# A transformer block on eight cores: layer norm steps spread over successive groups, and one matmul with ones per softmax total and per two query tiles

## The chip, the cores and the metric

One Trainium2 chip, eight cores. Each core takes one of the eight sequences (2048 tokens of width 2048) and all the weights, and runs the same program; no core waits for another. The metric is the time of one execution in microseconds, that of the slowest core. Lower is better.

## The reference

```python
xn = (x - mean) / sqrt(var + 1e-5)                 # x: (8, 2048, 2048)
Q = xn @ W_q; K = xn @ W_k; V = xn @ W_v           # 16 query heads, 4 key heads of 128
Qr, Kr = rope(Q), rope(K)
attn = softmax(Qr @ Kr.T / sqrt(128)) @ V; attn = attn @ W_o
gate = silu((xn @ w_gate) * s_gate)                # int8 weights, 2048 x 8192
up = (xn @ w_up) * s_up
ffn = ((gate * up) @ w_down) * s_down              # 8192 x 2048
out = x + attn + ffn
```

## The kernel before

The program is written out engine by engine. Each helper call appends an instruction, or a wait for a counter that another engine raises, to the list of one engine: "t" (TensorE, PE in the profile), "v" (VectorE, DVE), "s" (ScalarE, ACT), "g" (GpSimd, POOL, which also issues the casting weight loads) and "y" (SyncE, SP, which issues the other DMAs). Each engine takes its list strictly in order. Matmuls are recorded in two helper lines, L109 (inside a sum) and L113 (the last of a sum), so that a matmul is told by its tiles.

**Prologue.** The 2048 rows come in 16 tiles of 128 rows (`x_t`, four buffers). Of each, `ln_stats` (DVE, L368 and L371) takes mean and variance, `ln_scale` makes the factors (a square root on ACT at L377, a reciprocal and a product on DVE), `ln_apply` (ACT, L392) writes the normalised rows in bf16, and `ln_transpose` turns them into `xn`, features on partitions: 16 small matmuls against the identity into two PSUM banks `ps_t` (L405), which ACT (L413) or DVE (L411) copies out. `xn[t]` holds four such tiles, 512 tokens. `ln_stage(t, j)`, for j from 0 to 7, does this for the four tiles of one `xn[t]`: statistics in stages 0 to 3, factors for two tiles at a time, transposes in stages 4 to 7, each copied out by ACT alone.

Between the stages stand groups of 16 matmuls: `keys(t, g)` (one key head of 512 tokens, by `rotated`) and `v_rows(t, sub)` (128 tokens of V). `rotated` writes a bank; DVE multiplies it with the cosine and sine tables (L465 to L467), ACT squares it into `sqb` (L469), POOL adds the products into `kst` (L473), SP stores that. `norms` later issues one matmul of `sqb` with a matrix of ones into `ps_m` (the squared length of each token's vector, on all partitions) and a DVE maximum over it (L446): an upper bound for the softmax exponent. `v_rows` writes a half of `ps_s`, ACT copies it to one of two `vst` buffers (L489), SP stores it. After the first four key groups come 28 groups with the stages of tiles 8 to 15 between the first 16; then 64 query groups (16 heads of four 512-token tiles) with the same `rotated`.

**Main part.** Two passes over 1024 tokens each. In a pass the feed-forward network, in products of eight matmuls (`ps_f`, seven products for each 2x2 block product), is the outer loop. DVE and ACT combine and evacuate the products, POOL and DVE make the weight operands; `add_operands` (POOL, L299) is a load that adds to what is there, and waits for the load before it. Between the matmuls `attention` takes steps, STEPS of them over each pass, evenly by the count of matmuls. A softmax tile has eight steps: two score matmuls (`ps_s`), one exponential of 128x1024 on ACT (L990), two matmuls with V. The exponentials are summed in `acc`, by DVE in steps 1 and 2 and by POOL in steps 3 to 7 (L1007). At step 7 `split` (POOL) adds the halves of `acc` (L951), casts the result to bf16 (`hi`, L953) and takes the remainder (`lo`, L955). During the next tile, at step 4, `total` sums over the partitions by two matmuls with ones (`hi`, then `lo`) into `ps_m`; DVE inverts at steps 4 and 5 and multiplies at step 6. The passes end with the output projection. In the trace the attention of the two passes begins at 457 and 1986 us, their output projections at 1769 and 3288 us.

## Time and profile before

| | |
|---|---|
| median of three runs | 3573.27 us (3490.6 to 3616.72) |
| the profiled execution, its own time | 3487.79 us |
| its span, slowest core | 3486.1 us (the eight cores: 3471.1 to 3486.1) |
| PE busy in the span | 98% |
| outside the span | 1.7 us |

The profile is that of the core whose span is longest. Sums below are made against the profiled execution.

### The profile page before, as it was taken

The page shows a single profiled execution, that of the slowest core. Times are in us where ns is not written, and L with a number is a line of the kernel's source. Part 1 is how long each engine was busy: PE and PEld are TensorE (multiplying, and loading weights), DVE is VectorE, ACT ScalarE, POOL GpSimd, SP SyncE. Part 2 cuts the span into 40 slices and gives each one's busy share as a digit, 9 for nine tenths or more (in the row PEclk, how much of TensorE's full clock was granted, in tenths as well). Part 3 has the DMA queues.
Part 4 walks back from the last instruction along what each step waited for, and adds up shares of the span by engine and source line. Part 5 has one row for each costly group of instructions (what it writes and reads, how often), then busy time and mean ns, then how long its engine had stood idle before and what let it go on. Part 6 is the DMA issues. An engine that isn't in the chain of part 4 may idle for free.

```text
span 3486.1 us, 49034 instructions; the slowest of 8 cores (3471.1 to 3486.1 us)
## 1 busy us (share of the span) xinstructions
PE 3399.9 (98%) x15824; PEld 1542.6 (44%) x15824; DVE 2391.4 (69%) x3226; ACT 1205.7 (35%) x1437; POOL 1624.7 (47%) x1521
## 2 busy tenths in 40 slices
PE   5899999999999999999999999999999999999999
PEld 2444444444444444444444444444444444444444
DVE  5468777767776777677743677677776777677633
ACT  4421133443334333443311133443344333433111
POOL 1134445555555555555511155555555555555311
PEclk9999999999999999999999999999999999999999
DMA  8555476698668776667697666676667666676864
GB/s 214 156 114 145 152 209 181 169 151 170 181 179 144 155 191 178 143 143 195 183 225 124 145 180 184 150 169 176 183 153 164 176 181 154 142 183 181 210 127 85
DMA packets 180568, 578.98 MB, mean 166 GB/s; under 512 B 28256, under 2 KB 54880, under 8 KB 176096
## 3 DMA queue, kind: packets, MB, share of 16 engines
q0 software_dynamic: 132768, 484.53, 60.2%
q1 hardware_dynamic: 47552, 91.32, 8.2%
q8 instruction: 134, 2.20, 0.3%
q14 instruction: 114, 0.93, 0.1%
HBM read 318.64 MB, written 109.05 MB: 123 GB/s over the span
## 4 chain that ended last, share of the span: by engine, by line
PE 89%; DMA 4%; DVE 3%; issue 2%; ACT 1%; POOL 1%; DVEq 0%; POOLq 0%; ACTq 0%; SPq 0%
PE ps_f L109 54%; PE ps_f L113 8%; PE ps_s L109 7%; PE ps_av L109 6%; PE ps_k L109 4%; PE ps_s L113 3%; PE ps_av L113 3%; PE ps_m L109 2%; DMA x_t<-x_nat 1%; DMA wab<-wd 1%; PE ps_m L113 1%; DMA outT<-ost 1%; DVE st L368 1%; POOL kst L473 0%; ACT expT L990 0%
## 5 line engine op out<-in xcount | busy, mean ns | idle before, releaser
L109 PE MATMUL ps_f<-xop,wab 128*128 128x512 bf16 x6272 | 1545.2, 379 | 15.4 <-DVE th L750 7.1
L990 ACT ACTIVATE expT<-ps_s,bias,isq_sb 128x1024 bf16<-128x1024 f32 x512 | 616.6, 1204 | 1092.9 <-PE ps_s L113 1043.3
L1007 POOL TENSOR_TENSOR acc<-acc,expT 128x1024 f32<-128x1024 f32 x320 | 688.5, 2152 | 634.9 <-ACT expT L990 581.4
L109 PEld LDWEIGHTS ps_f<-xop,wab 128*128 128x128 bf16 x6272 | 612.1, 98 | 761.2 <-issue 28.2
L109 PE MATMUL ps_f<-fop,wab 128*128 128x512 bf16 x3136 | 770.8, 380 | 12.9 <-DVE fop L766 4.5
L109 PEld LDWEIGHTS ps_f<-fop,wab 128*128 128x128 bf16 x3136 | 306.8, 98 | 386.4 <-issue 19.6
L113 PE MATMUL ps_f<-xop,wab 128*128 128x512 bf16 x896 | 339.6, 379 | 0.0
L814 DVE TENSOR_TENSOR ps_f<-ps_f,usum 128x512 f32<-128x512 f32 x384 | 264.8, 690 | 72.1 <-PE ps_f L113 64.9
L791 ACT ACTIVATE ost<-ps_f,sd_sb 128x512 f32<-128x512 f32 x256 | 174.5, 686 | 306.6 <-DVE ps_f L814 195.4
L822 DVE TENSOR_TENSOR usum<-usum,ps_f 128x512 f32<-128x512 f32 x384 | 260.0, 677 | 13.3 <-PE ps_f L113 13.1
L745 ACT ACTIVATE th<-ps_f,sgh 128x512 f32<-128x512 f32 x256 | 170.4, 686 | 229.5 <-DVE ps_f L814 194.9
L854 DVE TENSOR_TENSOR usum<-m2c,ps_f 128x512 f32<-128x512 f32 x192 | 131.0, 682 | 167.9 <-PE ps_f L113 145.8
L968 DVE RECIPROCAL ps_m<-ps_m 128x256 f32<-128x256 f32 x128 | 225.0, 1758 | 29.2 <-PE ps_m L113 28.7
L640 POOL DMA_DIRECT2D outT<-ost x127 | 112.0, 944 | 283.9 <-DVE ost L702 150.2
L750 DVE SCALAR_TENSOR_TENSOR th<-th,ps_f 128x512 f32<-128x512 f32 x256 | 170.2, 682 | 105.4 <-ACT th L745 103.2
L473 POOL TENSOR_TENSOR kst<-rpa,rpb 128x512 bf16<-128x512 f32 x80 | 111.3, 1395 | 281.3 <-DVE rpb L467 194.5
L850 ACT ACTIVATE m2c<-ps_f 128x512 f32<-128x512 f32 x192 | 114.4, 596 | 320.8 <-PE ps_f L113 262.3
L862 DVE TENSOR_TENSOR usum<-usum,ps_f 128x512 f32<-128x512 f32 x192 | 131.5, 685 | 135.1 <-PE ps_f L113 132.2
L311 DVE TENSOR_TENSOR wab<-wab 128x1024 bf16<-128x1024 bf16 x192 | 192.5, 1003 | 40.1 <-DMA wab<-wd 25.9
L766 DVE SCALAR_TENSOR_TENSOR fop<-ps_f,sgu,th 128x512 bf16<-128x512 f32 x256 | 188.9, 744 | 25.9 <-PE ps_f L113 9.7
L113 PE MATMUL ps_av<-expT,vt 128*128 128x512 bf16 x512 | 194.3, 379 | 0.0
L109 PE MATMUL ps_av<-expT,vt 128*128 128x512 bf16 x512 | 194.3, 379 | 0.0
(116 smaller groups left out, 3782.9 us busy)
## 6 DMA issues: line engine op xcount, KB each, us to landing
wab<-wg POOLq DMA_DIRECT2D x299, 512.0 KB, 4.9
wab<-wu POOLq DMA_DIRECT2D x296, 512.0 KB, 4.9
wab<-wd POOLq DMA_DIRECT2D x146, 512.0 KB, 4.8
outT<-ost POOLq DMA_DIRECT2D x127, 512.0 KB, 7.7
x_t<-x_nat SPq DMA_DIRECT2D x16, 1024.0 KB, 9.2
wo_sb<-wo POOLq DMA_DIRECT2D x32, 512.0 KB, 9.4
ring<-wq POOLq DMA_DIRECT2D x16, 512.0 KB, 7.8
q_scr<-kst SPq DMA_DIRECT2D x64, 128.0 KB, 2.8
```

What stands on the lines that cost most here:

```text
L109: streams["t"].append(lambda t, o=out, l=lhsT, r=rhs, a=start, z=stop: t.matmul(o, l, r, start=a, stop=z, skip_group_check=True))
L113: return op("t", lambda t, o=out, l=lhsT, r=rhs, a=start, z=stop: t.matmul(o, l, r, start=a, stop=z, skip_group_check=True))
L311: build = lambda v: v.tensor_sub(w[:, WS1], w[:, W11], w[:, W22])
L745: tanh = op("s", lambda s: s.activation(th[k][:], src[:], AF.Tanh, scale=sgh[:, ic:ic + 1]))
L750: th_ready[k] = op("v", lambda v: v.scalar_tensor_tensor(th[k][:], th[k][:], 1.0, src[:], ALU.add, ALU.mult))
L766: th_free[k] = op("v", lambda v: v.scalar_tensor_tensor(fop[:, slot, i, :], src[:], sgu[:, ic:ic + 1], th[k][:], ALU.mult, ALU.mult))
L791: written = op("s", lambda s: s.activation(ost[b][:, tile, :], src[:], AF.Identity, scale=sd_sb[:, dc:dc + 1]))
L814: c = op("v", lambda v: v.tensor_tensor(ps_f[bank][:], ps_f[bank][:], U[:], sign))
L822: take = lambda v: v.tensor_sub(U[:], U[:], ps_f[bank][:])
L968: c["inverse"] = op("v", lambda v: v.reciprocal(ps_m[:, cols], ps_m[:, cols]))
L990: e = op("s", lambda s, kk=k, gg=g, rr=r, tt=t: s.activation(expT[:, kk, :], ps_s[:], AF.Exp, bias=bias[:, gg, rr, tt:tt + 1], scale=isq_s ...
L1007: summed = op(eng, lambda x, d=acc, o=one, kk=k: x.tensor_add(d[:], o, expT[:, kk, :]))
```

## The change

It has three parts.

**Layer norm and loads in the prologue.** `ln_stage` gives way to `look(i)` (statistics), `rows(i)` (factors and normalised rows) and `cols(i)` (transposes, copied out by ACT and DVE, a half each). They are placed one step per group in the order look, rows, cols of successive tiles. Factors are made for one tile at a time. The loads of tiles 8 to 11 are issued after the first two groups of the 28 instead of after each `ln_apply`, the load of V's weights waits for tile 5 instead of tile 7, and the tables for tokens 1024 and up are loaded later. `v_rows` has four `vst` buffers, and its copy and store stand ahead of the layer norm steps.

**Query norms.** For queries ACT squares the 128 rows of the bank in two halves of 64 rows, each into rows 0 to 63 or 64 to 127 of its own buffer by whether the tile is even or odd; POOL adds the two buffers once per two tiles; one matmul with `halves` (ones in the two diagonal 64x64 blocks) serves both. `finish_norms` puts the maxima back in place with four small DVE copies.

**Softmax totals.** At step 7 only the halves of `acc` are added (`fold`). In the next tile's step 1 ACT copies rows 64 to 127 of the sum beside rows 0 to 63 (`shift`), at step 2 POOL adds them and splits the 64 rows (`split`), at step 3 ACT copies `lo` into rows 64 to 127 of `hl` (`lower`), and at step 4 one matmul with ones takes both. STEPS is 263, for the three more steps at a pass's end.

```diff
-            def ln_stage(t, j):
...
-                if j >= 4:
-                    ln_transpose(i + j - 4, ("s", "s"))
...
+            def look(i):
+                def run():
+                    seen[i] = ln_stats(i)
+                return run
+            def rows(i):
+                def run():
+                    ln_apply(i, ln_scale(i // 2 % 2, i % 2, 1, seen[i]))
+                    if 8 <= i < 12:
+                        load_x(i + 4)
+                return run
+            def cols(i):
+                return lambda: ln_transpose(i, ("s", "v"))
...
-            ln_stage(1, 0)
-            ln_stage(1, 1)
-            keys(0, 0, [stage(1, 2), stage(1, 3)])
-            wait("g", x_loaded[7])
+            look(4)()
+            rows(4)()
+            keys(0, 0)
+            wait("g", x_loaded[5])
             wv_loaded = dma("g", l_wv, lambda g: g.dma_start(wv_sb[:], wvd))
-            keys(0, 1, [stage(1, 4)])
-            keys(0, 2, [stage(1, 5)])
-            ln_stage(1, 6)
-            keys(0, 3, [stage(1, 7)])
+            keys(0, 1, [cols(4), look(5)])
+            keys(0, 2, [rows(5), look(6)])
+            keys(0, 3, [cols(5), rows(6), look(7)])
+            rows(7)()
+            cols(6)()
+            cols(7)()
...
+            beside = {4: [look(8)], 5: [rows(8), look(9)], 6: [cols(8), rows(9), look(10)],
+                      7: [cols(9), rows(10), look(11)], 8: [cols(10), rows(11), look(12)],
+                      9: [cols(11), rows(12), look(13)], 10: [rows(13), look(14)], 11: [cols(12), rows(14), look(15)],
+                      12: [cols(13), rows(15)], 13: [cols(14)], 14: [cols(15)]}
             for n, (what, t, k) in enumerate(groups):
-                v_last = what(t, k, [stage(2 + n // 8, n % 8)] if n < 16 else ())
-                if n == 4:
-                    load_cs(2)
-                    load_cs(3)
-                if n == 11:
+                v_last = what(t, k, beside.get(n, ()))
+                if n < 2:
+                    load_x(2 * n + 8)
+                    load_x(2 * n + 9)
+                if n in (8, 13):
+                    load_cs(2 + n // 13)
+                if n == 13:
...
+                    k, at_ = (n * NT + t) // 2 % 2, t % 2 * 64
+                    wait("s", freed, sq_free[k])
+                    op("s", lambda s: s.activation(sqb[k][at_:at_ + 64, :], bank[0:64, :], AF.Square))
+                    squared = op("s", lambda s: s.activation(squ[k][at_:at_ + 64, :], bank[64:128, :], AF.Square))
...
+                if n >= G and t % 2:
+                    wait("g", squared)
+                    both = op("g", lambda g: g.tensor_add(sqb[k][:], sqb[k][:], squ[k][:]))
+                    behind.append((both, k, biggest, halves))
...
+            def fold(acc, summed):
                 wait("g", summed)
-                f = op("g", lambda g: g.tensor_add(acc[:, 0:TS], acc[:, 0:TS], acc[:, TS:]))
+                return op("g", lambda g: g.tensor_add(acc[:, 0:TS], acc[:, 0:TS], acc[:, TS:]))
+            def shift(c):
+                acc = c["acc"]
+                wait("s", c["sum"])
+                c["sum"] = op("s", lambda s: s.activation(acc[0:64, TS:], acc[64:128, 0:TS], AF.Copy))
+            def split(c):
+                acc = c["acc"]
+                wait("g", c["sum"])
+                f = op("g", lambda g: g.tensor_add(acc[0:64, 0:TS], acc[0:64, 0:TS], acc[0:64, TS:]))
...
+            def lower(c):
+                wait("s", c["low"], hl_free[0])
+                c["parts"] = op("s", lambda s: s.activation(hl[64:128, :], lo[0:64, :], AF.Copy))
...
-                mm(ps_m[:], ones[:], hi[:], True, False)
-                hl_free[0] = mm_last(ps_m[:], ones[:], lo[:], False, True)
+                hl_free[0] = mm_last(ps_m[:], ones[:], hl[:], True, True)
...
-            ending = {4: total, 5: lambda c: invert(c, 1), 6: normalise}
+            ending = {1: shift, 2: split, 3: lower, 4: total, 5: lambda c: invert(c, 1), 6: normalise}
```

How the instructions move, at three places. Numbers behind a name only tell buffers apart, and lines of the changed kernel lie higher (L405 becomes L411). First, PE in the first four key groups, before (`xn_tm0` is tile 4, `xn_tm1` tile 5):

```order
L109 MATMUL ps_k1<-xn0_70,ring2_54 128x512 x15
L113 MATMUL ps_k1<-xn0_70,ring2_54 128x512
L405 MATMUL ps_t0<-ident_sb_92,xn_tm0_65 128x128 x8
L405 MATMUL ps_t1<-ident_sb_92,xn_tm0_65 128x128 x8
L109 MATMUL ps_av<-xn0_70,ring3_55 128x512 x15
L113 MATMUL ps_av<-xn0_70,ring3_55 128x512
L113 MATMUL ps_m<-sqb0_86,ones_43 128x512
L405 MATMUL ps_t0<-ident_sb_92,xn_tm1_66 128x128 x8
L405 MATMUL ps_t1<-ident_sb_92,xn_tm1_66 128x128 x8
L405 MATMUL ps_t0<-ident_sb_92,xn_tm2_67 128x128 x8
L405 MATMUL ps_t1<-ident_sb_92,xn_tm2_67 128x128 x8
L109 MATMUL ps_k0<-xn0_70,ring4_56 128x512 x15
```

and in the changed kernel:

```order
L109 MATMUL ps_k1<-xn0_71,ring2_55 128x512 x15
L113 MATMUL ps_k1<-xn0_71,ring2_55 128x512
L411 MATMUL ps_t0<-ident_sb_97,xn_tm0_66 128x128 x8
L411 MATMUL ps_t1<-ident_sb_97,xn_tm0_66 128x128 x8
L109 MATMUL ps_av<-xn0_71,ring3_56 128x512 x15
L113 MATMUL ps_av<-xn0_71,ring3_56 128x512
L113 MATMUL ps_m<-sqb0_87,ones_43 128x512
L109 MATMUL ps_k0<-xn0_71,ring4_57 128x512 x15
L113 MATMUL ps_k0<-xn0_71,ring4_57 128x512
L113 MATMUL ps_m<-sqb1_88,ones_43 128x512
L411 MATMUL ps_t0<-ident_sb_97,xn_tm1_67 128x128 x8
L411 MATMUL ps_t1<-ident_sb_97,xn_tm1_67 128x128 x8
```

Tile 5's and tile 6's transposes stood ahead of the fourth key group (`ring4`); now they stand behind it. On SP over the same groups, before (`x_t0` to `x_t3` are tiles 8 to 11):

```order
L346 DMA sin_sb1_79<-sinT 128x512
L337 DMA x_t0_61<-x_nat 128x2048
L337 DMA x_t1_62<-x_nat 128x2048
L337 DMA x_t2_63<-x_nat 128x2048
L475 DMA k_scr<-kst0_88 128x512
L337 DMA x_t3_64<-x_nat 128x2048
L475 DMA k_scr<-kst1_89 128x512
L475 DMA k_scr<-kst0_88 128x512
L475 DMA k_scr<-kst1_89 128x512
```

and in the changed kernel:

```order
L352 DMA sin_sb1_80<-sinT 128x512
L492 DMA k_scr<-kst0_91 128x512
L492 DMA k_scr<-kst1_92 128x512
L492 DMA k_scr<-kst0_91 128x512
L492 DMA k_scr<-kst1_92 128x512
L563 DMA sg_sb_98<-sg 128x64
L563 DMA su_sb_99<-su 128x64
L563 DMA sd_sb_47<-sd 128x16
L492 DMA k_scr<-kst0_91 128x512
L343 DMA x_t0_62<-x_nat 128x2048
L343 DMA x_t1_63<-x_nat 128x2048
```

The loads of tiles 8 to 11 stood among the stores of the first key groups; now these stores and three small tables go first. Last, the end of a softmax tile. On POOL, before:

```order
L1007 TENSOR_TENSOR acc_0_125<-acc_0_125,expT_120 128x1024
L951 TENSOR_TENSOR acc_0_125<-acc_0_125 128x512
L953 CAST hi_127<-acc_0_125 128x512
L955 TENSOR_TENSOR lo_128<-acc_0_125,hi_127 128x512
L299 DMA wab0_59<-wg8 128x2048
L291 DMA wab1_60<-wu8 128x2048 x3
L299 DMA wab1_60<-wu8 128x2048 x2
L1007 TENSOR_TENSOR acc_1_126<-acc_1_126,expT_120 128x1024
```

and in the changed kernel:

```order
L1048 TENSOR_TENSOR acc_0_131<-acc_0_131,expT_126 128x1024
L977 TENSOR_TENSOR acc_0_131<-acc_0_131 128x512
L302 DMA wab1_61<-wu8 128x2048 x2
L294 DMA wab0_60<-wg8 128x2048 x3
L989 TENSOR_TENSOR acc_0_131<-acc_0_131 64x512
L991 CAST hl_133<-acc_0_131 64x512
L993 TENSOR_TENSOR lo_134<-acc_0_131,hl_133 64x512
L302 DMA wab0_60<-wg8 128x2048
L1048 TENSOR_TENSOR acc_1_132<-acc_1_132,expT_126 128x1024
```

The cast and the difference stood right behind the sum of the halves; now they stand five weight loads later, on 64 rows. On ACT over such a tile, before:

```order
L990 ACTIVATE expT_120<-ps_s,bias_50,isq_sb_47 128x1024
L945 ACTIVATE av_sb_129<-ps_av 128x512
L745 ACTIVATE th3_124<-ps_f3,sgh_44 128x512
L745 ACTIVATE th1_122<-ps_f0,sgh_44 128x512
L990 ACTIVATE expT_120<-ps_s,bias_50,isq_sb_47 128x1024
L745 ACTIVATE th2_123<-ps_f1,sgh_44 128x512
L990 ACTIVATE expT_120<-ps_s,bias_50,isq_sb_47 128x1024
L745 ACTIVATE th0_121<-ps_f2,sgh_44 128x512
L850 ACTIVATE m2c_109<-ps_f3 128x512
L990 ACTIVATE expT_120<-ps_s,bias_50,isq_sb_47 128x1024 x3
```

and in the changed kernel:

```order
L1031 ACTIVATE expT_126<-ps_s,bias_51,isq_sb_48 128x1024
L972 ACTIVATE av_sb_135<-ps_av 128x512
L1031 ACTIVATE expT_126<-ps_s,bias_51,isq_sb_48 128x1024
L984 ACTIVATE acc_0_131<-acc_0_131 64x512
L772 ACTIVATE th3_130<-ps_f3,sgh_45 128x512
L772 ACTIVATE th1_128<-ps_f0,sgh_45 128x512
L772 ACTIVATE th2_129<-ps_f1,sgh_45 128x512
L1031 ACTIVATE expT_126<-ps_s,bias_51,isq_sb_48 128x1024
L772 ACTIVATE th0_127<-ps_f2,sgh_45 128x512
L877 ACTIVATE m2c_115<-ps_f3 128x512
L1031 ACTIVATE expT_126<-ps_s,bias_51,isq_sb_48 128x1024
L998 ACTIVATE hl_133<-lo_134 64x512
L1031 ACTIVATE expT_126<-ps_s,bias_51,isq_sb_48 128x1024 x2
```

The copy of `acc` (L984, `shift`) now stands ahead of three tanh evacuations of the feed-forward network, and that of `lo` (L998, `lower`) behind another exponential.

## Rows read from the trace of the kernel before

**Rows 1.** The page, part 1: busy time of each engine, share, instructions

```profile
PE 3399.9 (98%) x15824; PEld 1542.6 (44%) x15824; DVE 2391.4 (69%) x3226; ACT 1205.7 (35%) x1437; POOL 1624.7 (47%) x1521
```

**Rows 2.** Windows: stretch; busy of PE, PEld, DVE, ACT, POOL; clock; DMA share, GB/s

```profile
31.12:71.69 40.57, 26.06 (x131) 12.96 (x131) 20.70 (x40) 17.63 (x17) 3.05 (x3) 0.79 0.88 228
71.69:196.81 125.12, 111.25 (x589) 53.29 (x590) 57.96 (x104) 48.38 (x56) 21.41 (x21) 0.96 0.57 148
196.81:436.37 239.56, 236.88 (x1097) 107.10 (x1096) 189.22 (x262) 47.34 (x70) 99.62 (x80) 1.00 0.51 137
436.37:1770.00 1333.63, 1316.37 (x6071) 593.61 (x6072) 975.48 (x1287) 511.40 (x601) 723.09 (x665) 1.00 0.73 175
1970.00:3290.00 1320.00, 1308.95 (x6057) 591.44 (x6056) 976.02 (x1287) 514.17 (x603) 722.34 (x664) 1.00 0.68 174
```

**Rows 3.** Timeline of PE, 49 to 140 us: start, duration, line, tiles, [idle before]

```profile
49.57 1.86 PE L405 MATMUL ps_t<-ident_sb,xn_tm 128*128 128x128 bf16 x16 [8.86 <-ACT xn_tm L392]
...
71.69 3.40 PE L109 MATMUL ps_k<-xn,ring 128*128 128x512 bf16 x15 [1.73 <-ACT xn L413]
...
104.04 0.61 PE L405 MATMUL ps_t<-ident_sb,xn_tm 128*128 128x128 bf16 x8 [4.79 <-ACT xn L413]
...
126.98 5.77 PE L109 MATMUL ps_s<-wv_sb,xn 128*128 128x512 bf16 x15 [4.38 <-ACT vst L489]
...
139.71 1.06 PE L405 MATMUL ps_t<-ident_sb,xn_tm 128*128 128x128 bf16 x16
```

**Rows 4.** Timeline of DVE and ACT, 43 to 60 us

```profile
43.24 2.47 DVE L368 BATCH_NORM_STATS2 st<-x_t 128x6 f32<-128x512 f32 x4 [9.52 <-DMA x_t<-x_nat]
...
46.17 0.30 ACT L377 ACTIVATE std<-mv,eps_sb 128x2 f32<-128x2 f32 x1 [15.73 <-DVE mv L371]
...
49.84 2.41 DVE L368 BATCH_NORM_STATS2 st<-x_t 128x6 f32<-128x512 f32 x4
...
53.63 0.68 DVE L465 TENSOR_TENSOR rpa<-ps_k,cos_sb 128x512 f32<-128x512 f32 x1
...
53.86 2.09 ACT L392 ACTIVATE xn_tm<-x_t,nmr,rstd 128x2048 bf16<-128x2048 f32 x1 [0.86 <-DVE nmr L383]
...
57.95 0.69 DVE L446 TENSOR_REDUCE kmaxs<-ps_m 128x1 f32<-128x512 f32 x1
...
58.33 1.93 ACT L413 ACTIVATE xn<-ps_t 128x1024 bf16<-128x1024 bf16 x2
```

**Rows 5.** Timeline of ACT, around 126 us

```profile
126.24 0.60 ACT L489 ACTIVATE vst<-ps_s 128x512 bf16<-128x512 f32 x1 [8.47 <-DMA v_scr<-vst]
```

**Rows 6.** Timeline of PE, 428 to 437 us: end of the query projections

```profile
428.58 3.40 PE L109 MATMUL ps_k<-xn,ring 128*128 128x512 bf16 x15
...
431.82 0.38 PE L113 MATMUL ps_k<-xn,ring 128*128 128x512 bf16 x1
...
436.37 0.38 PE L113 MATMUL ps_m<-sqb,ones 128*128 128x512 bf16 x1 [2.01 <-ACT sqb L469]
```

**Rows 7.** Groups by line and shape on POOL: busy, mean ns, idle before

```profile
L299 POOL DMA_DIRECT2D wab<-wu x112 | 98.2, 896 | 111.2 <-DMA wab<-wu 108.5 <-PE ps_f L113 2.7
...
L951 POOL TENSOR_TENSOR acc<-acc 128x512 f32<-128x512 f32 x64 | 87.8, 1372 | 9.2
...
L955 POOL TENSOR_TENSOR lo<-acc,hi 128x512 bf16<-128x512 f32 x64 | 76.7, 1199 | 9.3
```

**Rows 8.** Timeline of POOL and ACT, 926 to 944 us: end of a softmax tile

```profile
926.91 1.27 POOL L951 TENSOR_TENSOR acc<-acc 128x512 f32<-128x512 f32 x1
...
932.63 1.20 ACT L990 ACTIVATE expT<-ps_s,bias,isq_sb 128x1024 bf16<-128x1024 f32 x1 [2.78 <-PE ps_s L113]
...
942.35 1.21 ACT L990 ACTIVATE expT<-ps_s,bias,isq_sb 128x1024 bf16<-128x1024 f32 x1
```

**Rows 9.** Waits of PE, 197 us to the end: total, times, longest

```profile
PE ps_f L109 <- DVE th L750: 10.3, 11, 1.6
...
PE ps_m L113 <- ACT sqb L469: 2.7, 2, 2.0
```

More of the change, by code:

```diff
@@ L225, in build_program @@
         l_kst = lanes("kst", 2)
-        l_vst = lanes("vst", 2)
+        l_vst = lanes("vst", 4)
         l_spill = lanes("spill", 2)
@@ L614, in finish_norms @@
                 wait("v", m_free[0])
+                for t in range(2):
+                    for k in (0, 64):
+                        last = op("v", lambda v, a=64 * t, t=t, k=k: v.tensor_copy(
+                            qmaxs[k:k + 64, :, :, t::2], qmax2[a:a + 64]))
+                wait("v", last)
                 kmax_ready = op("v", lambda v: v.reduce_max(kmax[:], kmaxs[:], axis=AX.X))
```

70 lines of the change are left out of this document (30 added, 40 removed).

## The prediction

> **What bounds the kernel now.** I begin with the page's busy times: PE is busy for 3399.9 of 3486.1 us [rows 1], so two things only can shorten the run: fewer matmuls, and fewer of the 86 us in which PE stands still or runs at half its clock. The windows say where those are [rows 2]. From 31.12 to 71.69 us PE has work for 26.1 of 40.6 us, at a mean granted clock of 0.79. From 71.69 us, where the first key group of tokens 512 to 1023 starts, to 196.81 us, where the query projections start, it has 111.3 of 125.1 us at 0.96. In the query projections it is idle for 2.7 us of 239.6, in the two attention stretches for 17.3 and 11.1 us at full clock. So in everything behind 197 us PE is the bound and a matmul taken away is worth its own time; ahead of it, order is what matters. The timeline of PE names the waits of the prologue [rows 3]: 8.86 us ahead of tile 4's transposes, 4.79 us inside tile 9's, 4.38 us ahead of a V group that waits for `vst`.
>
> **A matmul's price.** Fifteen matmuls start at 428.58 and the closing one at 431.82 [rows 6]: 3.24 / 15 = 0.216 us from start to start. The 0.38 of a row is the modelled length, not the price. A group of 16 is 3.46 us.
>
> **Prologue to the start at 71.69.** Tile 4's transposes wait, before, for the factors of tiles 4 and 5 together, and tile 5 arrives at 43.24 [rows 4]. In the changed kernel tile 4 goes alone and that wait ends; but what is late next is tiles 5 to 7 themselves. The group that starts at 71.69 needs all four. From 43.24 the list of DVE holds up to tile 7's factors: three statistics (2.47 and an aggregate: 2.8 each, 8.4), three triples of rope products (0.68 x 3, 6.2), two maxima of 0.69 (1.4), one copy out of PSUM (0.7, taken like the maximum) and three sets of factors at 1.2 (0.30 for the root and 0.86 until the rows are written, 3.6) [rows 4]. Sum 20.3, so 63.5 us. Then ACT: tile 7's rows 2.09, the waiting half of tile 6's copy 0.97 (half of 1.93), tile 7's first transposes 0.5 and its copy 1.0: 68.1 us. Gain 3.6 us. Tiles 6 and 7 don't bind unless late: the statistics of tile 7 started at 49.84 with no idle ahead of it [rows 4], so it had landed, and DVE now asks for it at about 57.
>
> PE will have been nearly idle before 68.1, where it now comes from a busy stretch. The row nearest to this is the V group after 4.38 us of idle: its 15 matmuls took 5.77 against 3.40 us for 15 at full clock [rows 3, 6], so 2.4 us lost. I take 2.4 (between 0 and 3.4, the time at half clock of one more group). Net gain at the start 1.2.
>
> **71.69 to 196.81.** At full clock the work is 28 groups x 16 x 0.216 = 96.8, eight sets of transposes at 0.90 (the row has 1.06, less the 0.16 by which a modelled end passes the next start) = 7.2, and twelve norms of 0.216 = 2.6: 106.6 us of 125.1. The other 18.5 are waits (13.9 by the window) and half clock. What caused them: statistics ahead of the rope products of the same group, ACT doing both halves of a tile's copy, and `vst` blocked for 8.47 us behind the store queue [rows 5], where an x load stood before each store. All three go: four `vst` buffers, one DVE half, and in the V groups, which have no rope products, the statistics. What comes next is ACT: per group with transposes it now has the copy of V 0.60, a root 0.30, 0.86 until the factors are there, the rows 2.09 and half a tile 0.97, in all 4.82 us [rows 4, 5] against PE's 3.46 + 0.90 = 4.36. Eight such groups lose 0.46 each: 3.7 us. That gives 110.3, a gain of 14.8. Bounds: 18.5 if the buffers hide ACT, 7 if half of the old waits stay. The moved instructions cost SP little: the key stores now go ahead of tile 8's load, which is asked for at about 85 us and issued at about 76; a load of this size has all of DMA's share that V's weights left (V's weights start when tile 5 is there, not tile 7).
>
> **Query projections.** 32 norm matmuls fewer: 32 x 0.216 = 6.9 us. Added per query tile is one more ACT square (0.60, as for a copy of this width [rows 5]) and per two tiles one POOL add (1.37, the nearest row in rows 7, though that one is f32). ACT is busy for 47 and POOL for 100 of 240 us [rows 2], so with 38 and 44 more they fit. Two places lose: PE waits for `sqb` twice, 2.7 us in all [rows 9]. The last one, 2.01 us at the end of the projections [rows 6], now waits for a second square and the POOL add: 2.0 more. At the other, a bank is freed by the second square: 0.6 more. Sum: 6.9 - 2.6 = 4.3 (bounds 2 and 7).
>
> **Softmax totals.** 64 tiles x 0.216 = 13.8 us of PE. What is added is on ACT and POOL: per tile two ACT copies (0.6 each) and one POOL add (1.27 [rows 8]). ACT has 511 busy of 1334 us [rows 2] and 39 more, POOL 723 and 41 more. `shift` waits for the sum of the halves: this ends at 926.91 + 1.27 = 928.2, the exponential of step 1 at 933.8 [rows 8], 5.6 us later: never late. `lower` waits for `split`, which starts at about step 2's matmuls, 937, and takes 1.27 + 0.6 + 1.2 [rows 7, 8], to 940.1, against the end of step 3's exponential at 943.6: 3.4 us to spare. Behind these waits on ACT are the tanh evacuations, for which DVE and then PE wait. PE's own waits for that chain are 10.3 us in 11 places [rows 9]; a copy ahead of it lengthens it by 0.6, in a fraction of the tiles. I take 3 us (5 of 64 tiles lose 0.6; bounds -3, since the cast and difference no longer stand ahead of weight loads, and 19, half of the tiles). Net 10.8.
>
> **The sum.** 1.2 + 14.8 + 4.3 + 10.8 = 31.1 us off the profiled execution's 3487.8: **3457 us**, 0.9% less. I forecast for executions like the profiled one, which lies at the low end of the three runs shown (3490.6 to 3616.7); against their median of 3573 the same number would look like 3%, and that would be no effect of the change. The memsets of `halves` hide behind the first loads of x and `finish_norms`' four copies behind PE's first four banks; uncovered, the copies would cost less than four maxima, 4 x 0.69 = 2.8 us.
>
> **A rule beside the rows.** The sum of halves on POOL has a mean of 1.37 us over 64 [rows 7] and 1.27 us undisturbed [rows 8], so 0.10 us a piece goes to others, 6 us in all, in 28 us of PE's idle time. The Trainium skill, "SBUF — State Buffer", section "SBUF: two separate sides", has GpSimd and VectorE share a port pair by an exclusive lock: an instruction of VectorE with two SBUF inputs and one of GpSimd that reads SBUF don't overlap. By that rule alone every added POOL add could stop VectorE for its full length. The rows speak for a tenth of it. Were the whole length lost, 64 x 1.27 = 81 us would fall on DVE, which has 358 + 344 us free in the two stretches [rows 2]; if PE paid half, the time would be 3457 + 40 = 3497. I give this 2 in 100.
>
> **Rivals.** *The saved matmuls turn into waits.* ACT's copies stand ahead of the evacuations in half of the tiles and PE loses 0.6 in each: 19 us instead of 3, 3473. For it: PE already waits there in 11 places. Against: ACT is idle for 60% of these stretches. *The prologue gains less.* V's weights now load beside tiles 6 and 7, and DMA's share is already 0.88 there [rows 2]. If tile 7 comes at 69 us instead of by 49.8 (12 us after DVE asks for it), everything behind moves by 12: 3469. *More gain.* ACT's rhythm is hidden, the clock returns at once and POOL's relief takes waits away: 3.7 + 2.4 + 6 + 3 = 15 more, 3442. *Slower than before.* POOL takes its list in order, and L299's loads wait for the load before them, 108.5 us over 112 of them [rows 7], 1 us on average. Where `split` stands behind such a wait of more than the 3.4 us to spare, ACT stops in `lower`, and with it exponentials and tanh. It decides from 31 / 64 = 0.5 us per tile on; at 1 us per tile the time is 3457 + 64 = 3521. Against: it takes waits four times the mean in every tile.
>
> **How the numbers follow.** Forecast (3445 to 3466) 0.64, waits in the attention 0.14, less in the prologue 0.08, more gain 0.08, slower through POOL 0.04, the port 0.02. The range of 8 in 10 goes from 3438 (beyond the case of more gain) to 3479 (beyond the two that lose part). Two per cent, about what a measurement of this kernel can tell from no change, is 70 us: faster by that would need twice the forecast gain, 0.03; slower would need the stop in `lower` at 1.6 us or more per tile, 0.02; within it 0.95.
>
> **What the changed profile would show.** PE with 96 matmuls fewer and no wait ahead of tile 4's transposes; the group of tokens 512 on starting at about 68 us, its first matmuls at half clock; the query projections starting at about 180 us; one wait of about 4 us at their end; `ps_m<-hl` 64 times, no long wait of ACT for `lo`; PE idle in each attention stretch within a few us of 17 and 11. The prediction is wrong if the idle time of those stretches grows by more than 10 us each, or if the projections start after 187 us.

## The result, and the profile after

| | before | changed |
|---|---|---|
| executions, four each | 3487.89 to 3616.72 us | 3450.99 to 4023.58 us |
| median | 3531.93 us | 3645.41 us |
| ratio of comparable executions | | 0.9892, 95% interval 0.9863 to 0.9921 |
| the profiled execution | 3487.79 us | 3452.65 us |
| PE in its slowest core | 3399.9 of 3486.1 us | 3376.9 of 3451.1 us |

The change makes the kernel 1.1% faster, within the 2% that count as the same. In some executions of either kernel all cores of a die run at a lower granted clock (0.84 to 0.89 in the two of the changed one that took 3838 and 4024 us, by which alone the medians say the opposite), so the ratio leaves these executions out, "mean span" below takes only cores of a die whose clock was 0.994 or more, and "cores 4 to 7" below means these alone, because cores 0 to 3 of that chip had 0.986 to 0.995 with the kernel before as well. The changed kernel run again gave 3449.12 to 3450.84 us in four executions, ratio 0.989 (0.9875 to 0.9904).

The profile is that of core 1. First the page's busy times, as [rows 1]:

```profile
PE 3376.9 (98%) x15728; PEld 1531.9 (44%) x15728; DVE 2420.4 (70%) x3216; ACT 1317.8 (38%) x1623; POOL 1765.3 (51%) x1620
```

96 matmuls fewer, 23 us less of PE; ACT has 112 us more, POOL 141, DVE 29. The windows of the stages, columns as in [rows 2]:

```profile
31.31:68.36 37.05, 22.57 (x131) 11.92 (x132) 23.92 (x46) 15.47 (x16) 5.53 (x5) 0.79 0.81 176
68.36:180.20 111.84, 110.31 (x592) 52.81 (x593) 63.92 (x115) 41.49 (x52) 18.82 (x19) 0.98 0.79 187
180.20:416.00 235.80, 229.38 (x1058) 103.02 (x1057) 164.73 (x227) 83.28 (x131) 127.43 (x110) 1.00 0.55 138
416.00:1741.00 1325.00, 1311.37 (x6043) 591.32 (x6042) 1001.06 (x1295) 555.31 (x668) 779.98 (x698) 1.00 0.73 175
1941.00:3253.00 1312.00, 1300.89 (x6019) 587.59 (x6017) 994.29 (x1287) 554.95 (x666) 776.27 (x695) 1.00 0.70 175
```

PE's idle time is 14.5 us ahead of 68.36 (as before) and 1.5 us in the next stretch (before 13.9). The window of the query projections ends here at 416, ahead of their last norm at 420.62, while the one in [rows 2] ends with it. Cut as there, at 179.73, 420.62 and 1741, PE is idle for 9.6 us in the query projections (before 2.7) and for 10.4 in the first attention stretch (before 17.3); in the second it is 11.1 as before. The timeline of PE in the prologue, against [rows 3]:

```profile
40.54 1.06 PE L411 MATMUL ps_t<-ident_sb,xn_tm 128*128 128x128 bf16 x16
...
51.10 1.05 PE L411 MATMUL ps_t<-ident_sb,xn_tm 128*128 128x128 bf16 x16 [1.82 <-ACT xn_tm L398]
58.25 1.87 PE L411 MATMUL ps_t<-ident_sb,xn_tm 128*128 128x128 bf16 x16 [6.10 <-ACT xn_tm L398]
65.55 1.86 PE L411 MATMUL ps_t<-ident_sb,xn_tm 128*128 128x128 bf16 x16 [5.43 <-ACT xn L419]
68.36 5.97 PE L109 MATMUL ps_k<-xn,ring 128*128 128x512 bf16 x15 [0.94 <-DVE xn L417]
...
96.73 1.05 PE L411 MATMUL ps_t<-ident_sb,xn_tm 128*128 128x128 bf16 x16 [0.40 <-ACT xn_tm L398]
...
101.62 1.05 PE L411 MATMUL ps_t<-ident_sb,xn_tm 128*128 128x128 bf16 x16 [0.38 <-ACT xn_tm L398]
...
106.50 1.05 PE L411 MATMUL ps_t<-ident_sb,xn_tm 128*128 128x128 bf16 x16 [0.38 <-ACT xn_tm L398]
...
111.38 0.83 PE L411 MATMUL ps_t<-ident_sb,xn_tm 128*128 128x128 bf16 x12 [0.38 <-ACT xn_tm L398]
```

Tile 4's transposes at 40.54 wait for nothing. Those of tiles 5, 6 and 7 wait 1.82, 6.10 and 5.43 us: the wait has gone down the row of tiles. Tokens 512 to 1023 begin at 68.36 us, at half clock (granted 0.50 from 60 to 71.5 us, in the first eight of which PE was busy for 2.0; 15 matmuls in 5.97 us against 3.40). From 96.73 on, four transposes in a row wait 0.38 to 0.40 us each for the rows that ACT writes, 4.88 us apart; behind them PE waits for nothing until the query projections, whose first matmul is at 179.73. There (PE again, against [rows 6]):

```profile
206.06 3.40 PE L109 MATMUL ps_av<-xn,ring 128*128 128x512 bf16 x15 [1.34 <-ACT squ L483]
...
236.30 3.40 PE L109 MATMUL ps_k<-xn,ring 128*128 128x512 bf16 x15 [0.76 <-ACT squ L483]
...
420.62 0.38 PE L113 MATMUL ps_m<-sqb,halves 128*128 128x512 bf16 x1 [3.21 <-POOL sqb L489]
```

The first two are matmuls that wait for a bank which the second square (L483) frees; there are five of that kind, 4.4 us in all. The last is the closing norm behind POOL's sum, 3.21 us for 2.01 before. PE's waits and one of ACT's from 197 us on, as [rows 9]:

```profile
PE ps_f L109 <- DVE th L777: 11.9, 12, 1.8
...
PE ps_m L113 <- POOL sqb L489: 5.1, 4, 3.2
...
ACT hl L998 <- POOL lo L993: 3.9, 2, 2.0
```

**Stages, mean of eight cores.** The profiled execution of every run has a trace of each core. The stages below are read from PE's rows on all of them: the first matmul of the query projections; from it to their last norm matmul; from that to the first matmul of the second output projection. "Mean span" is over all executions of the run, with an uncertainty of 0.3 to 1.1 us, and is set against the same mean of the kernel before (3478.2 to 3480.3 us), for "changed" that of its one traced execution, for the others that of several on the same chip.

| kernel | query projections start | they last, to the last norm | attention, to the second output projection | mean span, difference |
|---|---|---|---|---|
| before | 194.0 | 239.6 | 2846.0 | |
| changed | 179.3 | 236.3 | 2829.4 | -35.4 |
| changed, again | 179.6 | 234.9 | 2829.1 | -37.5 |
| prologue alone | 179.8 | 239.9 | 2845.1 | -16.7 |
| query norms alone | 195.2 | 237.4 | 2846.6 | -3.1 |
| softmax totals alone | 194.3 | 239.6 | 2831.8 | -13.2 |

### The profile page after: what moved, and what is told of

Its sections match the earlier page's. It is cut to its first block, busy times and chain, and to the rows that moved or that the text cites. A ratio compares the mean times of both kernels' runs of the same rounds, so it can differ in the third digit from the quotient of the medians.

```text
span 3451.1 us, 49221 instructions; the slowest of 8 cores (3436.1 to 3451.1 us)
## 1 busy us (share of the span) xinstructions
PE 3376.9 (98%) x15728; PEld 1531.9 (44%) x15728; DVE 2420.4 (70%) x3216; ACT 1317.8 (38%) x1623; POOL 1765.3 (51%) x1620
## 4 chain that ended last, share of the span: by engine, by line
PE 93%; DVE 2%; DMA 2%; issue 2%; ACT 1%; POOL 1%; DVEq 0%; ACTq 0%; POOLq 0%; SPq 0%
PE ps_f L109 57%; PE ps_f L113 8%; PE ps_s L109 7%; PE ps_av L109 6%; PE ps_k L109 4%; PE ps_s L113 3%; PE ps_av L113 3%; PE ps_m L109 2%; DMA q_scr<-kst 1%; PE ps_m L113 1%; PE ps_t L411 0%; ACT xn_tm L398 0%; POOL kst L486 0%; DMA wab<-wd 0%; PE ps_k L113 0%
## 5 line engine op out<-in xcount | busy, mean ns | idle before, releaser
L1048 POOL TENSOR_TENSOR acc<-acc,expT 128x1024 f32<-128x1024 f32 x320 | 688.5, 2152 | 553.5 <-ACT expT L1031 512.6
L849 DVE TENSOR_TENSOR usum<-usum,ps_f 128x512 f32<-128x512 f32 x384 | 259.9, 677 | 11.0 <-PE ps_f L113 11.0
L800 DVE TENSOR_TENSOR fop<-fop 128x512 bf16<-128x512 bf16 x320 | 200.6, 659 | 6.7
L109 PE MATMUL ps_s<-qr,kr 128*128 128x512 bf16 x512 | 194.3, 379 | 0.8 <-ACT expT L1031 0.8
## 6 DMA issues: line engine op xcount, KB each, us to landing
x_t<-x_nat SPq DMA_DIRECT2D x16, 1024.0 KB, 10.8
```

The costliest lines, as they stand in the source:

```text
L109: streams["t"].append(lambda t, o=out, l=lhsT, r=rhs, a=start, z=stop: t.matmul(o, l, r, start=a, stop=z, skip_group_check=True))
L800: fop_ready[dst] = op("v", lambda v: v.tensor_tensor(fop[:, dst, i, :], fop[:, one, i, :], fop[:, two, i, :], how))
L849: take = lambda v: v.tensor_sub(U[:], U[:], ps_f[bank][:])
L1048: summed = op(eng, lambda x, d=acc, o=one, kk=k: x.tensor_add(d[:], o, expT[:, kk, :]))
```

## The experiments

### The three parts one by one

Each is the kernel before with one part of the diff and nothing else (STEPS 263 with the softmax part, 260 without).

> The prologue's part of the change alone (layer norm steps spread, loads in order of use, four vst buffers); query norms and softmax totals as before. If the parts add up, the query projections start 15 to 17 us earlier than before (medians over the cores) and nothing behind changes by more than 1 us: about 3472 us. Rival: part of the gain is given back later, because V's weights and the later x loads push the stores; then the projections start early and the end moves by less than 12 us.

Ratio 0.994 (0.992 to 0.9959), -16.7 us.

> The query norms' part alone. By the prediction 4.3 us less in the query projections (32 matmuls are 6.9 us, less 2.6 of longer waits): about 3484 us. By the profile of the changed kernel 2 to 3 us less, because PE waits for a bank until ACT's second square five times, where DVE adds the xn halves into xop, and for the last POOL add.

Ratio 0.9985 (0.9974 to 0.9997), -3.1 us.

> The softmax totals' part alone. By the prediction 10.8 us less (13.8 from 64 matmuls, less 3 for two more ACT copies per tile): about 3477 us. Rival: the copies cost nothing and POOL is relieved, since its cast and difference no longer stand ahead of the weight loads: 14 to 17 us less, about 3472 us.

Ratio 0.9954 (0.9938 to 0.997), -13.2 us.

The three add up to -33.0 us and the product of the ratios is 0.9879, against -35.4 and -37.5 us and 0.9892 for all together. By the ratios nothing is missing; by mean spans the sum is 2 to 4 us short, with an uncertainty of nearly 2. In the table each part moves its own column most, but the last two less than in the whole: the norms 2.2 us of 3.3 and 4.7, the totals 14.2 of 16.6 and 16.8. So no part costs another anything, and a small gain comes perhaps only in company; the waits in the attention, below, point that way. The prologue part is the largest, as forecast.

### Inside the prologue: buffers or order

The kernel before with four `vst` buffers and the copy of V ahead of the layer norm steps:

```diff
-        vst = [place("vst%d" % i, ...) for i in range(2)]
+        vst = [place("vst%d" % i, ...) for i in range(4)]
...
+                wait("s", done, vs_free[sub])
+                s_free[vb] = op("s", lambda s: s.activation(vst[sub][:], ps_s[:, vb, :], AF.Copy))
...
                 for f in between:
                     f()
-                wait("s", done, vs_free[vb])
-                s_free[vb] = op("s", lambda s: s.activation(vst[vb][:], ps_s[:, vb, :], AF.Copy))
```

> The kernel before with four vst buffers and the copy and store of V ahead of the layer norm steps, nothing else of the change. The wait of 4.4 us for vst goes, with it the half clock behind it (2.4 us): projections start 5 to 7 us earlier if that wait was last, less than 2 us if the layer norm of the next tiles holds PE instead.

Ratio 0.9977 (0.9964 to 0.999), -7.6 us; the projections start at 186.6 us, half of the part's gain. The other way round, the changed kernel with two buffers and the copy behind the steps:

> The changed kernel with two buffers for V rows instead of four, and with their copy and store again behind the layer norm steps: the order of layer norm steps and of loads alone. The buffers alone had moved the start of the query projections from about 196 to 187 us, the whole prologue part to 180. Theory (the two halves add): the projections start at about 188 us here, so 8 us of the 16 are lost and the ratio is 0.9892 + 0.0023 = 0.9915; PE waits again for vst. Rival 1 (with x loads out of the store queue the old buffers don't block any more): start near 181, ratio 0.9895. Rival 2 (both are needed, each wait takes the place of the other): start near 193, ratio 0.993.

Ratio 0.9929 (0.9913 to 0.9945). Of cores 4 to 7 the mean span is 35.2 us below before, and the projections start at 180.2 (the changed kernel's, on the same cores of its two traced executions, at 178.9 and 179.7). So rival 1 holds for the start, and the ratio's own size, nearer to rival 2, comes from cores 0 to 3: with the new order the buffers are worth 0 to 2 us. They are a second cure of the same wait: on the timeline of PE (core 5) one wait for `vst` of 0.86 us is left of [rows 3]'s 4.38.

```profile
106.17 1.05 PE L411 MATMUL ps_t<-ident_sb,xn_tm 128*128 128x128 bf16 x16 [0.38 <-ACT xn_tm L398]
...
111.05 1.05 PE L411 MATMUL ps_t<-ident_sb,xn_tm 128*128 128x128 bf16 x16 [0.38 <-ACT xn_tm L398]
...
116.42 3.40 PE L109 MATMUL ps_s<-wv_sb,xn 128*128 128x512 bf16 x15 [0.86 <-ACT vst L506]
```

Changed with the loads of tiles 8 to 11 issued after each tile's rows, as before:

```diff
-                    if 8 <= i < 12:
+                    if 4 <= i < 12:
                         load_x(i + 4)
...
-                if n < 2:
-                    load_x(2 * n + 8)
-                    load_x(2 * n + 9)
```

> The changed kernel with the x loads issued after each ln_apply again, as before, all else kept (steps, vst, V's weights). If the place of the loads matters by itself, the load of tile 8 and later stand ahead of V's weights and the key stores, kst is held and the projections start 3 us or more later than in the changed kernel (180 us). If the order of the steps and the vst buffers make the gain, the start of the projections stays within 1 us.

Ratio 0.9886 (0.9857 to 0.9914), mean span 3442.7 us, the changed kernel's 3442.5 to 3442.8. On cores 2 to 5 of its traced execution the projections start at 178.2 to 180.2 us, as the expectation without an effect has it (the other four cores can't be compared). The place of these loads is worth nothing; it was not combined with two buffers, so whether the loads would block those again stays open. What does bind is ACT. Both halves of a transposed tile copied by ACT, as before the change (`("s", "s")` in `cols`):

> The changed kernel with both halves of each transposed tile copied out by ACT, as before the change, where the change gives one half to DVE. My forecast had ACT as the next bound of the stretch (4.82 us per group against PE's 4.36). If that holds, 0.97 us more per group on ACT goes straight to PE in eight groups: 8 us later, query projections at about 188 us, ratio 0.9915. Rival: ACT is not the bound (PE waited for nothing between 112 us and the projections), four buffers give slack, and the cost is 0 to 2 us: ratio 0.989 to 0.9898.

Ratio 0.9916 (0.9897 to 0.9935); of cores 4 to 7 the mean span is 33.0 us below before, 2 to 4 us of the gain lost, and the projections start at 181.3. Between the two expectations, and the timeline of PE (core 5) shows why:

```profile
94.99 1.05 PE L411 MATMUL ps_t<-ident_sb,xn_tm 128*128 128x128 bf16 x16 [0.40 <-ACT xn_tm L398]
...
100.78 1.05 PE L411 MATMUL ps_t<-ident_sb,xn_tm 128*128 128x128 bf16 x16 [1.29 <-ACT xn_tm L398]
...
106.58 1.05 PE L411 MATMUL ps_t<-ident_sb,xn_tm 128*128 128x128 bf16 x16 [1.29 <-ACT xn_tm L398]
...
112.38 1.05 PE L411 MATMUL ps_t<-ident_sb,xn_tm 128*128 128x128 bf16 x16 [1.29 <-ACT xn_tm L398]
```

The groups are 5.80 us apart where they were 4.88: ACT's rhythm is the forecast's 4.82 plus the 0.97 of another half, so in these groups ACT does set the pace. But there are only four in a row with a wait, not eight, and 3 x 0.92 = 2.8 us is what is lost.

### Query norms: banks and the end

```diff
+                if n == G and t == 0:
+                    banks.extend([ps_s[:, 0, :], ps_s[:, 1, :]])
+                    bank_free.extend([(s_free[0],), (s_free[1],)])
```

> The changed kernel with five instead of three PSUM banks for the query groups (the two halves of ps_s, idle then, are added). If PE's waits for ACT's second square come from the banks, all of them go (4.4 us in five places in the changed kernel's trace) and the projections take 4 us less; waits for POOL's add stay. Rival: DVE's sums of xn are what is late, and the waits move to the norm matmuls: less than 2 us gained. About 3448 us or 3451.

Ratio 0.9884 (0.9855 to 0.9912), mean span 3440.2 us, 2.3 and 2.6 below the two runs of the changed kernel. The projections last 234.2 us, and no wait for `squ` is left on any core; in the changed kernel these waits are 2.4 us in the mean of eight cores, in its second run 1.5. So the gain is what these waits had cost, between the two expectations. Then also the last two tiles' norms one by one, with `ones`, as for keys:

> The changed kernel with five PSUM banks in turn in the query projections and with the norms of the last two query tiles taken alone, as for keys. Theory: what the query projections still lose is two things only, the bank that the second square frees late (2.3 us less with five banks) and the wait for the POOL add at their end (3.2 us where it was 2.0 before the change). Both gone, the projections last about 226.5 us against 230.1 and the ratio to the kernel before is 0.9883 (3447 us). Rival: the last wait is not the POOL add but whatever closes the projections (rope, store, maxima); then the wait of about 3.5 us stays and the ratio is that of five banks alone plus one matmul more, 0.9885 to 0.989.

Ratio 0.9907 (0.989 to 0.9925), -35.1 us by cores 4 to 7: no better than the changed kernel, and rather worse than five banks (-39.1). Neither expectation was right. The timelines of PE and DVE at the end (core 4):

```profile
412.63 0.38 PE L113 MATMUL ps_m<-sqb,ones 128*128 128x512 bf16 x1 [4.24 <-DVE qmaxs L452]
```

```profile
408.72 0.68 DVE L477 TENSOR_TENSOR rpb<-ps_s,sin_sb 64x512 f32<-64x512 f32 x1
409.44 2.32 DVE L653 COPY qmaxs<-qmax 64x16 f32<-64x16 f32 x12
411.79 0.69 DVE L452 TENSOR_REDUCE qmaxs<-ps_m 128x1 f32<-128x512 f32 x1
```

My edit put the twelve small copies of the maxima (L653, 2.32 us) between two maxima on DVE; there is one `ps_m`, and the last norm waits 4.24 us for it, on every core, for 3.21 in the changed kernel. The wait was replaced by one of my own making, so what the POOL sum costs at the end was not isolated.

### Softmax totals: the copies and the place

The copies on ACT twice each (128 instructions more, each waited for):

```diff
             def shift(c):
...
+                wait("s", op("s", lambda s: s.activation(acc[0:64, TS:], acc[64:128, 0:TS], AF.Copy)))
...
             def lower(c):
...
+                wait("s", op("s", lambda s: s.activation(hl[64:128, :], lo[0:64, :], AF.Copy)))
```

> The changed kernel with shift and lower each done twice on ACT (the second right behind the first, with a wait of ACT for itself), so 128 more ACT copies of 0.63 us and nothing else. If an ACT copy ahead of the tanh evacuations costs PE what the prediction took (3 us for 128), the attention takes 3 us more than in the changed kernel; if its cost was hidden in the 13.8 us of the saved matmuls and POOL's relief masked it, 6 to 8 us more: 3460 us; if ACT has room, the time is that of the changed kernel within 1 us.

Ratio 0.9895 (0.9872 to 0.9917), mean span 3444.1 +- 0.8, attention 2828.6 us for 2829.4 and 2829.1. By mean spans, 80 us more on ACT cost between nothing and 2.3 us (-35.2 us against the kernel before, for -35.4 and -37.5).

The kernel before with `split` at step 2 of the next tile and all else as it was (128 rows, two matmuls):

```diff
-            ending = {4: total, 5: lambda c: invert(c, 1), 6: normalise}
+            ending = {2: split, 4: total, 5: lambda c: invert(c, 1), 6: normalise}
```

> The kernel before, with only the place of the split changed: the halves are added at step 7, the cast to bf16 and the difference (128 rows, as before) come at step 2 of the next tile, no ACT copies, two matmuls with ones as before. If the relief of POOL is worth something by itself, PE's idle time in the attention falls and the time is 2 to 4 us less than before, and POOL waits less for the adding weight loads (190 us before). If only the matmuls count, the time is that of before within 1 us.

Ratio 0.9975 (0.9962 to 0.9988), -5.8 us without one matmul less. STEPS is 261 here for 260, which the diff does not show, so all steps of the attention lie a little differently between the matmuls. PE's waits between 440 and 3290 us, mean of eight cores, fall from 25.2 to 20.6 us. The adding loads (L299) can't be shown to be the reason: see the next run. It is the changed kernel with the split moved forward, from step 2 to step 0 of the next tile (and STEPS 261 for 263):

```diff
-            ending = {1: shift, 2: split, 3: lower, 4: total, 5: ..., 6: normalise}
+            def early(c):
+                shift(c)
+                split(c)
+            ending = {1: lower, 4: total, 5: ..., 6: normalise}
...
                             closing = dict(pending, av=evacuate(av_done))
+                            early(closing)
```

> The changed kernel with the split moved from step 2 of the next tile right behind the sum of the halves (the copy of 64 rows, the 64-row add, the cast and the remainder follow at once, with nothing of POOL between); one matmul with ones per tile as in the changed kernel. It has the same matmuls, so what it loses is what the late place was worth. Theory: the late split took POOL's cast and remainder out of the way of the adding weight loads and of the sums of the next tile, and was worth 4 to 9 us (the kernel before with this alone: 0.9975); here then 4 to 9 us are lost, ratio 0.9905 to 0.992, and POOL's waits for adding loads go from 93 back towards 150 to 190 us. Rival: the late place is worth nothing once there are only 64 rows to split; ratio 0.9885 to 0.9897, waits of POOL near 93 us or without effect on PE. A third: POOL now stands in a wait for ACT's copy at each tile's end, 1 us or more per tile reaches PE: ratio over 1.0.

The edit does less than that: `early` stands behind step 0 of the next tile, not at step 7, and in 58 of 64 tiles POOL issues one to three weight loads between the sum of the halves (L977) and the split (L989), where the changed kernel has about five. Ratio 0.9909 (0.989 to 0.9928); cores 4 to 7 are 40.6 us below before. My theory, that the late place itself is worth something, had it slower than the changed kernel by 4 to 9. Since this rests on four cores, both were run again on one chip:

> The changed kernel once more, as the yardstick for the two runs beside it on the same chip. Means over the cores of undisturbed dies have it 35 to 37 us below the kernel before so far (3442.8 against 3478 to 3480), a ratio of 0.9895. If the three parts only add, their single gains of 16.7, 3.1 and 13.2 us give 33.0, ratio 0.9905; the difference of 3 us between sum and whole is what this run can settle.

> The changed kernel with the split right behind the sum of the halves, once more beside the changed kernel. Theory (late place worth nothing or costs): it is 3 to 5 us faster than the changed kernel, as the cores 4 to 7 of the first run had it (40.6 us below the kernel before), most of it behind 440 us. Rival: that was one chip's state, and the two are equal within 1 us. The old theory, that the late place is worth 4 to 9 us, would have it slower by that.

Changed again: ratio 0.989, mean span 3442.5 +- 0.4. Early: 3445.13 and 3446.02 us against 3449.12 to 3450.84, too few comparable executions for a ratio, mean span 3439.8 +- 0.4. So the early place is 2.7 us faster, and the theory falls. What the different STEPS has in it was not tested. The adding loads don't decide either: in the changed kernel POOL's waits for adding loads are 93 us late and 128 us early (core 1 of the first run of each), and the one with more of them is the faster. The groups by line and shape, 440 to 3290 us, show what the late place costs (busy, mean ns | idle before); the changed kernel, core 1:

```profile
L800 DVE TENSOR_TENSOR fop<-fop 128x512 bf16<-128x512 bf16 x320 | 200.6, 659 | 6.7
...
L989 POOL TENSOR_TENSOR acc<-acc 64x512 f32<-64x512 f32 x64 | 93.7, 1463 | 19.8 <-ACT acc L984 19.3
L993 POOL TENSOR_TENSOR lo<-acc,hl 64x512 bf16<-64x512 f32 x64 | 89.5, 1399 | 9.3
...
L1048 DVE TENSOR_TENSOR acc<-acc,expT 128x1024 f32<-128x1024 f32 x64 | 86.9, 1358 | 56.5 <-ACT expT L1031 56.3
...
L991 POOL CAST hl<-acc 64x512 bf16<-64x512 f32 x64 | 55.2, 862 | 8.8 <-POOL acc L989 0.4
...
L984 ACT ACTIVATE acc<-acc 64x512 f32<-64x512 f32 x64 | 40.2, 628 | 1.6
L998 ACT ACTIVATE hl<-lo 64x512 bf16<-64x512 bf16 x64 | 40.2, 628 | 5.4 <-POOL lo L993 3.9
```

and the early split:

```profile
L800 DVE TENSOR_TENSOR fop<-fop 128x512 bf16<-128x512 bf16 x320 | 185.0, 610 | 6.7
...
L989 POOL TENSOR_TENSOR acc<-acc 64x512 f32<-64x512 f32 x64 | 83.7, 1307 | 76.0 <-ACT acc L984 76.0
L1052 DVE TENSOR_TENSOR acc<-acc,expT 128x1024 f32<-128x1024 f32 x64 | 78.3, 1223 | 65.4 <-ACT expT L1035 65.4
L993 POOL TENSOR_TENSOR lo<-acc,hl 64x512 bf16<-64x512 f32 x64 | 76.4, 1193 | 9.3
...
L991 POOL CAST hl<-acc 64x512 bf16<-64x512 f32 x64 | 46.1, 721 | 8.5
```

Early, the 64-row sum takes 1307 ns, the cast 721 and the remainder 1193; late, 1463, 862 and 1399. DVE's sums next to them lengthen too: `fop` from 610 to 659 ns, `acc` with two inputs of step 2 from 1223 to 1358; only that of step 1 (not shown) is shorter, 1230 for 1322. Late, `split` meets more of DVE's work, and both pay: 32 us of POOL's time over 64 tiles, and 16 + 9 - 6 = 19 of DVE's. That is 0.50 us per tile on POOL and 0.29 on DVE.

These means mix two kinds of instructions, and single rows show what happens. DVE's `fop` sum alone, then one that starts while POOL's sum into `acc` is running (changed kernel, core 1):

```profile
655.15 0.41 DVE L800 TENSOR_TENSOR fop<-fop 128x512 bf16<-128x512 bf16 x1
...
923.16 2.12 POOL L1048 TENSOR_TENSOR acc<-acc,expT 128x1024 f32<-128x1024 f32 x1 [1.98 <-ACT expT L1031]
923.43 0.68 DVE L849 TENSOR_TENSOR usum<-usum,ps_f 128x512 f32<-128x512 f32 x1
924.03 1.54 DVE L800 TENSOR_TENSOR fop<-fop 128x512 bf16<-128x512 bf16 x1
```

POOL's sum ends at 925.28, the `fop` sum at 925.57. Of the 320 `fop` sums of this core, 212 meet no sum and no cast of POOL and take 0.42 us. 45 begin while an L1048 of POOL is running and meet nothing else of POOL; all of them end 0.28 to 0.35 us behind its end, whether 0.1 or 2.1 us of it were left. `usum` (L849), one of whose inputs lies in PSUM, takes its usual 0.68 us beside it. This is the rule of the Trainium skill ("SBUF — State Buffer", "SBUF: two separate sides") that an instruction of VectorE with two SBUF inputs and one of GpSimd that reads SBUF don't overlap, and the trace agrees in full: whichever is second waits for the first. (POOL's turn to wait: a remainder L993 that begins with 1.20 us of a DVE sum left takes 2.22 us for 1.15 alone.) The price per tile is a part of `split`'s 3.2 us only because most of it meets no such instruction of DVE. The price is not new either: in the kernel before, `fop` sums (L773) have a mean of 609 ns for 0.42 alone, 61 us in all; in the changed kernel it is 77, with the early split 61 again. PE's waits on core 5, changed kernel and early split:

```profile
PE ps_f L109 <- DVE th L777: 12.0, 12, 1.8
...
PE ps_f L109 <- DVE fop L793: 6.0, 4, 2.4
```

```profile
PE ps_f L109 <- DVE th L777: 11.3, 12, 1.8
...
PE ps_f L109 <- DVE fop L793: 4.3, 2, 2.4
```

All of PE's waits in the attention sum to 20.4 and 17.2 us, mean of eight cores. That DVE's longer sums make this difference fits the rows, but the run moves STEPS as well, so it is not shown. The last run takes both edits that helped:

> The changed kernel with both edits that were better than it: five PSUM banks in turn in the query projections, and the split right behind the sum of the halves. Five banks alone took 2.6 us off the changed kernel by the means of the cores, the early split 3 to 5. They lie in different stretches; if they add, this is 6 to 7 us below the changed kernel and 43 us below the kernel before, ratio 0.9877 (mean of cores 3436 us). Rival: in the attention the kernel before's block products wait at the same places anyway, and the early split's gain does not come again: 2.6 us below the changed kernel, ratio 0.9888.

Ratio 0.9878 (0.9862 to 0.9895), executions from 3442.55 to 3450.39 us, mean span 3438.1 +- 1.0: 4.4 below the changed kernel, where 5.3 is the sum of the two. It is the fastest version here by mean span, by little: its gain over the early split alone, 1.7 us, is not beyond the uncertainty.

## Why the prediction was right or wrong

**The number as reported: wrong, and the step that failed is the last one, from the sum to a range with chances.** The prediction is made "for executions like the profiled one", its range is 3438 to 3479, and its six chances add up to 1.00 within such executions. Executions that take longer whatever the change got no term and no chance, though two of the three times shown for the kernel before (3573, 3617) were such. What came in its place: two of the four executions of the changed kernel took 3838 and 4024 us, so the median is 3645.41. For the others the forecast of 3457 stands 4.3 us above the profiled 3452.65 and 6 to 8 above the ones measured again, its ratio 0.9912 inside the first interval and just outside the second. Little of this is luck: by the terms below the forecast is 1.3 to 1.7 us too high ahead of the query projections and 6 too low in the attention, and these misses cancel only in small part.

**By its terms**, measured as differences of the stage means:

| | forecast | measured |
|---|---|---|
| start of tokens 512 on, and the stretch to the projections | -1.2 - 14.8 = -16.0 | -14.7, -14.3 |
| query projections, to their last norm | -4.3 | -3.3, -4.7 |
| softmax totals | -10.8 | -16.6, -16.8 |
| sum | -31.1 | -34.6, -35.9 |

**The start.** 68.1 us was forecast and 68.36 measured, by the chain that was added up, half clock included (2.6 us lost for 2.4). But the 3.6 us ahead of it were no gain of the change: [rows 3] is core 7, where this group starts at 71.69; on the other seven it started at 65.7 to 68.1, and the mean of eight went from 67.3 to 68.1. A single core's trace was taken for the kernel. **The stretch.** 110.3 + 2.4 us was forecast, 111.84 measured. The ACT rhythm is right (4.82, measured 4.88), but it was charged for eight groups, and only four transposes wait for ACT, 1.5 us in all. What the prediction held to be one cure with three causes is two that overlap: the order alone gives all but 0 to 2 us, the buffers alone half.

**Query projections.** Right in the sum. Banks freed by the second square cost 1.3 to 4.4 us on the eight cores, 2.4 in the mean and 1.5 in the second run (0.6 was forecast); the end costs 1.2 more, not 2.0.

**Softmax totals.** This term was mis-sized, by 6 us, and the step in it that failed is the sign of PE's waits. The 13.8 us for the matmuls stand. The prediction let two ACT copies per tile lengthen PE's waits by 3 us. Measured, twice as many copies cost 0 to 2.3 us, and PE's waits between the last norm and the second output projection fall, from 25.2 us to 20.0 and 20.4 (mean of eight cores). 3.6 us of that are waits that every core has before, two each and on one core three, and that none has after (core 5 before, 440 to 3290 us):

```profile
PE ps_f L109 <- DVE usum L854: 3.5, 2, 1.8
```

They are gone with the softmax part alone too, but there waits for `wab` grow from 1.7 to 2.8 us and the sum only falls to 23.5; in the changed kernel they are 1.0. That is the one place found where the whole gains more than its parts, from one traced execution of each. 13.8 and 5 make 19, 2 us more than measured; these were not found.

Why the waits fall stays open. A bound of -3 stood in the prediction for the cast and difference that no longer stand ahead of weight loads, and moving them away from step 7 alone was worth 5.8 us. That fits all runs, the early split too, which puts at least one weight load ahead of them in most tiles and has the lowest waits of all (17.2 us); but no run has one matmul per total with the split left at step 7. Every one of these runs also has another STEPS than the kernel before (261 or 263 for 260), and no run moved STEPS alone. *Slower through POOL* did not come: ACT waited for `lo` twice, 3.9 us in all. *The port*: the reading of its row was wrong. POOL's own sum, 0.10 us over its undisturbed length, shows only the cases in which POOL came second. Where it comes first DVE waits, and that stands in DVE's rows: the two groups of DVE sums shown above have 16 and 9 us more than in the kernel before, 0.4 us per tile. So the rule holds at full length where two such instructions meet, and the 2 in 100 for 3497 was fair only because they seldom do.

## What to carry to other kernels

A forecast for one kind of execution needs a second number, or a chance, for the other kinds that the times shown already contain. Take the start of a stage from all cores, since the profiled one is by choice the slowest and its lateness may be its own. Where a kernel's bound engine is 98% busy, removed matmuls return about their full price (13.2 to 14.2 us of 13.8 for the totals alone), unless what replaces them holds a buffer that the engine needs (3.1 of 6.9 for the norms); two more copies per tile on an engine at 40% cost next to nothing. When work is moved from one place of a periodic schedule to another, keep the count of steps or move it alone in a run of its own. And look for the cost of a conflict in the rows of both engines.

## What the runs showed of the hardware

A POOL instruction on 64 partitions takes as long as one on 128. The medians over 64 of each, early split against the kernel before: the sum 1.26 us against 1.27, the cast 0.60 against 0.61, the remainder 1.15 against 1.16. The same holds on ACT: 593 ns for a 64x512 square against 597 for 128x512. Halving the rows saves no time there, and only PE gained. The forecast had charged full length for them, and rightly. Not expected was how completely two engines' sums exclude each other: a DVE sum with both inputs in SBUF (0.42 us) that starts beside a POOL sum ends 0.28 us or a little more behind the end of that sum, after up to 2.35 us, while one with an input in PSUM keeps its 0.68.
